# New instruction orders for all engines in the landmark-attention block of a two-block transformer kernel

## The chip, the cores and the metric

The kernel runs on one core of one Trainium2 chip. Its work is spread over the core's engines: TensorE (PE in the profile, with its weight loads as PEld), VectorE (DVE), ScalarE (ACT), GpSimd (POOL) and SyncE (SP), which issues most of the DMAs. The metric is the device time of one execution in microseconds (us); lower is better.

## The reference

Eight batches of 512 rows with 256 features pass through four layers, each added to its input after a layer norm:

```python
x = x + _L0_attn_a_ref(_layernorm(x), ...)   # cluster attention, 16 heads of 16
x = x + _L0_ffn_ref(_layernorm(x), ...)      # 8 experts, top 1, weighted by the softmax's maximum
x = x + _L0_attn_b_ref(_layernorm(x), ...)   # landmark attention, 64 landmarks
x = x + _L0_ffn_ref(_layernorm(x), ...)      # the same experts again
```

The landmark attention, with which the change deals, is this (its rows are seen as 8 batches of 512):

```python
q = q / scale
k_lm = k.reshape(Bb, H, m, Nn // m, hd).mean(axis=-2)
q_lm = q.reshape(Bb, H, m, Nn // m, hd).mean(axis=-2)
kernel1 = softmax(einsum('bhnd,bhmd->bhnm', q, k_lm))
kernel2 = softmax(einsum('bhld,bhmd->bhlm', q_lm, k_lm))
kernel3 = softmax(einsum('bhmd,bhnd->bhmn', q_lm, k))
SV = kernel1 @ iterative_inv(kernel2) @ (kernel3 @ v)
# iterative_inv: V = K.T / denom, then six times
#   KV = K @ V;  V = 0.25 * V @ (13 I - KV @ (15 I - KV @ (7 I - KV)))
```

The expert layer sends each row to one expert: a router gives the expert, a running sum gives the row's place in a table sorted by expert, the rows are scattered there, multiplied tile by tile with their expert's matrix, stored, gathered back and added.

## The kernel before

Everything is float32, and X (all 4096 rows) stays in SBUF. The program has two blocks that follow each other. The first, `cluster_attention`, does the cluster attention of batches 0 to 7 and the first expert layer of batches 0 to 3 (group `m0`), and begins that of batches 4 to 7 (group `m1`). The second, `landmark_attention`, does the landmark attention of batches 0 to 7, the rest of `m1`, and the second expert layer: group `m2` (batches 0 to 3), `m3` (batches 4 to 6), and `d7` (batch 7, which multiplies with all experts and so needs no scatter).

In each block every engine walks through a list of its own, a string of items in the tables `CLUSTER_ORDER` and `LANDMARK_ORDER`. An item is a batch (or group), a dot and a step; the code of a step stands once for each engine that takes part in it. Engines work strictly in the order of their lists and meet by semaphores, so an item whose input is late holds back all that stands behind it on its engine. An accumulator bank is handed out in the order in which TensorE claims it (six banks in a ring for the second block), so that the order of claims is also an order of waits.

The steps of a batch `n` in the second block, with the line of the profile where the text needs it:

- `xn`, `xT`, `q`, `k`, `v`: layer norm (DVE L1293), transposes (PE L1535), projections (PE L1540, L1546) and their copies by ACT. The layer norm's scales for batch 4 stand inside `4.xn` on DVE and wait for rows that `m1` has combined.
- `S2`, `e2`, `m2`, `kT`, `d`, `A`: kernel2, its softmax and the start of the inverse. `e2` is ACT L1443; `A` fills `b_aw`.
- `sc`, `ec`, `tc`, `w`: kernel3 by pairs of heads: scores (PE L1582), maximum (DVE L1350), exponential (ACT L1455), transposes and their copy (PE L1589, ACT L1460), product with v (PE L1596).
- `sa`, `ea`, `na`, `ta`: kernel1 in eight units: scores (PE L1610), maximum (DVE L1363) and a copy to SBUF (ACT L1470), subtraction (POOL L1247), exponential (ACT L1474), sum (DVE L1368) and division (POOL L1256), transposes (PE L1618) and their copy (ACT L1478).
- `R` and `N` with `U`, `Q`, `D`: the six rounds of the inverse, for all 16 heads at once in one pair of banks (`b_inverse`). `R` is the square KV (PE L1633), then DVE makes `b_uq` (L1379, L1388), ACT copies the square in three parts (L1498, L1505) and POOL subtracts (L1267, into `b_tm`); `N` is the second product (PE L1646) and DVE's update of `b_aw` (L1398). The rounds of one batch, and the batches behind each other, form one serial chain.
- `Z`, `sv`, `pj`: the inverse is applied (PE L1654, DVE L1407), multiplied with kernel1 (PE L1660, ACT L1507), projected (PE L1666), added to X and measured for the next layer norm (DVE L1416, L1418).
- `idle0`, `idle1`: three small products of the identity each (L1526 to L1528), whose results nobody reads.

The steps of a group: `ln`, `rn`, `rx`, `lg`, `lt` (norm, transposes, router logits), `c1`, `c2`, `s1` to `s4` on DVE (places; `s3` ends with `f_pos`, L403), `sc` on POOL (one indirect DMA per tile of 128 rows, L307), `ld` on SP (fetch), `tt` and `ty` (transposes and the product with the expert's matrix, PE L582 and L593), `st` (store), `ga` on POOL (one indirect DMA per tile, L318), `bi` (biases), `co` on DVE (combining, L455, which frees the row buffer that the sixth gather behind it needs).

Three lines say how a list is used and how a scatter waits:

```python
for n, item in plan["pool"]:
    body(item, n, n % 2 if isinstance(n, int) else None)
...
    if int(i) == 0:
        pool.wait_ge(self.s_clean, self.cleaned)
        self.placed.wait(pool, label)
```

## Time and profile before

| | us |
|---|---|
| median of three executions (lowest, highest) | 1116.17 (1111.09, 1122.37) |
| profiled execution, its own time | 1124.09 |
| span of that execution in the trace | 1121.9 |
| first instruction of the second block in the trace | 422.96 |
| mean granted TensorE clock, share of full speed | 0.925 |
| span of the second block | 699 |

The profiled execution took 2.2 us more than its span, which is what lies before the first and behind the last instruction, and 7.9 us more than the median. All that the change touches lies in the last 699 us of the span.

### The profile page before, as it was taken

The numbers are of one execution on the slowest core, as the hardware profiler recorded it, in microseconds if no ns is written. First come the engines' busy times: TensorE is split into PE (matmuls) and PEld (weight loads), VectorE is DVE, ScalarE is ACT, GpSimd is POOL, SyncE is SP. The second block draws the span as 40 slices with busy tenths as digits, with TensorE's granted clock in tenths as the row PEclk, the third lists the DMA queues.
The fourth block names the chain that finished last, engine by engine and source line by source line (L and its number), as shares of the span: only waits on it lengthen the run. The fifth ranks groups of instructions, "written<-read, shape, count | busy, mean of one in ns | idle before, by whom it ended". The sixth has DMA issues, their size and how long they took to land. (4 is left out here: it accounts for less than half of the span.)

```text
span 1121.9 us, 37263 instructions
## 1 busy us (share of the span) xinstructions
PE 933.2 (83%) x15213; PEld 666.9 (59%) x15213; DVE 831.1 (74%) x2089; ACT 641.6 (57%) x1387; POOL 472.3 (42%) x443
## 2 busy tenths in 40 slices
PE   7899989998989888677888986597689989772898
...
DMA packets 51079, 61.71 MB, mean 55 GB/s; under 512 B 5601, under 2 KB 46177, under 8 KB 50913
## 3 DMA queue, kind: packets, MB, share of 16 engines
...
## 5 line engine op out<-in xcount | busy, mean ns | idle before, releaser
L764 POOL TENSOR_TENSOR a_pr<-a_pr,a_smax 128x512 f32<-128x512 f32 x128 | 133.3, 1042 | 177.5 <-DVE a_smax L877 168.0
L1267 POOL TENSOR_TENSOR b_tm<-b_aw,b_sq 128x640 f32<-128x640 f32 (+1 forms) x48 | 65.4, 1362 | 148.9 <-ACT b_sq L1505 143.5
L871 DVE TENSOR_TENSOR a_pr<-a_bank,a_mask 128x512 f32<-128x512 f32 x128 | 82.8, 682 | 42.0 <-PE a_bank L1066 34.7
L963 ACT ACTIVATE a_pr<-a_pr 128x512 f32<-128x512 f32 x128 | 78.6, 630 | 51.9 <-POOL a_pr L764 44.1
L1247 POOL TENSOR_TENSOR b_pa<-b_pa,b_amax 128x512 f32<-128x512 f32 x64 | 67.1, 1048 | 70.3 <-ACT b_pa L1470 61.8
L969 ACT ACTIVATE a_pT<-a_bank 128x512 f32<-128x512 f32 x128 | 71.1, 596 | 41.2 <-PE a_bank L1075 30.0
L1075 PE MATMUL a_bank<-ident,a_pr 128*128 128x128 f32 x512 | 76.4, 289 | 20.2 <-ACT a_pr L963 17.6
L1256 POOL TENSOR_TENSOR b_pa<-b_pa,b_asum 128x512 f32<-128x512 f32 x64 | 66.7, 1043 | 58.4 <-DVE b_asum L1371 54.2
L307 POOL DMA_INDIRECT rows_sorted<-f_rows,f_pos x60 | 58.2, 969 | 72.2 <-DVE f_pos L403 53.8
L1398 DVE SCALAR_TENSOR_TENSOR b_aw<-b_tm,b_inverse 128x320 f32<-128x320 f32 (+1 forms) x144 | 63.4, 440 | 33.1 <-PE b_inverse L1646 13.7
L318 POOL DMA_INDIRECT f_rows<-results_sorted,f_pos x60 | 58.6, 977 | 66.9 <-issue 34.4
L877 DVE TENSOR_REDUCE a_smax<-a_pr 128x4 f32<-128x512 f32 x128 | 82.3, 675 | 0.4
L1075 PEld LDWEIGHTS a_bank<-ident,a_pr 128*128 128x128 f32 x512 | 60.2, 147 | 36.6 <-issue 34.2
L1633 PE MATMUL b_inverse<-b_aw 64*64 64x80 f32 x1536 | 44.8, 252 | 35.9 <-DVE b_aw L1398 26.9
L593 PE MATMUL b_bank<-experts_w,f_xgT 128*128 x260 | 69.5, 400 | 2.7 <-issue 1.7
L1646 PE MATMUL b_inverse<-b_uq,b_sq 64*64 64x80 f32 (+1 forms) x1536 | 40.2, 244 | 37.8 <-DVE b_uq L1388 35.9
L1633 PEld LDWEIGHTS b_inverse<-b_aw 64*64 64x64 f32 x1536 | 36.5, 146 | 50.9 <-issue 50.4
L1540 PE MATMUL b_bank<-b_xT,qkv_w 128*128 128x512 f32 x128 | 62.0, 626 | 3.2 <-ACT b_xT L1431 2.4
L1646 PEld LDWEIGHTS b_inverse<-b_uq,b_sq 64*64 64x64 f32 x1536 | 33.3, 144 | 51.1 <-issue 50.8
L1455 ACT ACTIVATE b_pc<-b_bank,b_nmax 128x512 f32<-128x512 f32 x64 | 43.4, 687 | 31.0 <-DVE b_nmax L1350 10.6
L1019 PE MATMUL a_bank<-a_xT,a_wqkT 128*128 128x512 f32 x128 | 59.9, 600 | 0.0
L1088 PE MATMUL a_bank<-a_V,a_pT 128*32 128x17 f32 x4096 | 48.7, 188 | 11.1 <-issue 10.9
...
## 6 DMA issues: line engine op xcount, KB each, us to landing
...
rows_sorted<-f_rows,f_pos POOLq DMA_INDIRECT x60
f_rows<-results_sorted,f_pos POOLq DMA_INDIRECT x60
```

What stands on the lines that cost most here:

```text
L593: last = mm(gb[:, 0:C], self.xgT[:, k % 3, kc, :], ew[:, kc, bass.ds(e, 1), :], start=(kc == 0), stop=(kc == 1))
L764: nc.gpsimd.tensor_tensor(out=pr[:, u % AHEAD], in0=pr[:, u % AHEAD], in1=smax[:, u % AHEAD, :].unsqueeze(2).broadcast_to([P, HQ, KEYS]), ...
L871: pre.emptied(V_.tensor_tensor(out=pr[:, u % AHEAD], in0=gb[:].rearrange("p (h k) -> p h k", h=HQ), in1=mask[:, u // 4, :].unsqueeze(1).br ...
L877: V_.tensor_reduce(out=smax[:, u % AHEAD, :], in_=pr[:, u % AHEAD], axis=AX.X, op=ALU.max)\
L963: nc.scalar.activation(pr[:, u % AHEAD], pr[:, u % AHEAD], ACT.Exp, scale=float(HD) ** -0.5)\
L969: pre.emptied(nc.scalar.activation(pT[:, u % TURNED], gb[:].rearrange("p (h q) -> p h q", h=HQ), ACT.Copy), n, item)
L1075: last = nc.tensor.transpose(gb[:, h * P:(h + 1) * P], pr[:, u % AHEAD, h, :], ident[:])
L1247: nc.gpsimd.tensor_tensor(out=p, in0=p, in1=amax[:, (n * NA + u) % AHEAD].unsqueeze(2).broadcast_to([P, H8, M]), op=ALU.subtract).then_inc ...
L1256: nc.gpsimd.tensor_tensor(out=p, in0=p, in1=asum[:, (n * NA + u) % AHEAD, 1].unsqueeze(2).broadcast_to([P, H8, M]), op=ALU.mult).then_inc( ...
L1267: nc.gpsimd.tensor_tensor(out=tm[:, a:b, k], in0=aw3[:, a:b, k], in1=sq[:, a:b, k], op=ALU.subtract).then_inc(s_tm, 1)
L1633: last = mm(products[lands(s, e), s, 0:AW], aw[r, par, s, 0:M], aw[r, par, s, :], start=True, stop=True)
L1646: last = mm(products[lands(s, e), s, k], sq[r, s, 0:M], uq[r, s, k], start=True, stop=True)
```

## The change

Only the table `LANDMARK_ORDER` is new; no step's code is touched, and the first block is as it was. Every engine has the same items as before, in another order. (The number of rows below differs by a few only because neighbours that are alike are shown as one.)
```diff
 LANDMARK_ORDER = {
     "pe": """
-        0.idle0 0.xT0 0.xT1 0.q0 0.k0 m1.rx3.0 0.q1 m1.rx3.1 0.k1 0.v0 0.v1 0.S20 0.S21 0.S22 m1.lg3 0.S23 0.idle1
...
+        0.xT0 0.xT1 0.q0 0.k0 0.q1 0.idle0 0.k1 0.idle1 0.v0 0.v1 m1.rx3.0 1.idle0 m1.rx3.1 0.S20 0.S21 0.S22 0.S23
...
```

**TensorE, from the end of batch 3 to the first products of batch 4.** Before:

```order
L1654 MATMUL b_bank<-b_aw,b_k2n 64x16 x16
L1660 MATMUL b_bank<-b_p1T,b_zbd 32x512 x8
L1666 MATMUL b_bank<-landmarks_proj,b_svT 128x256 x6
L1535 MATMUL b_bank<-ident,b_xn 128x128 x4
L1666 MATMUL b_bank<-landmarks_proj,b_svT 128x256 x2
L1535 MATMUL b_bank<-ident,b_xn 128x128 x4
L1540 MATMUL b_bank<-b_xT,qkv_w 128x512 x8
```

Now:

```order
L1654 MATMUL b_bank<-b_aw,b_k2n 64x16 x16
L1660 MATMUL b_bank<-b_p1T,b_zbd 32x512 x8
L1535 MATMUL b_bank<-ident,b_xn 128x128 x8
L1666 MATMUL b_bank<-landmarks_proj,b_svT 128x256 x8
L1540 MATMUL b_bank<-b_xT,qkv_w 128x512 x8
L1546 MATMUL b_bank<-qkv_w,b_xT 128x256 x8
```

The transposes of batch 4 stand ahead of batch 3's projection instead of in it and behind it.

**TensorE, around the place where the positions of group `m2` are computed** (L551 and L552 are `m2.s2`; L1633 is `4.R0`, L1646 `4.N0`). Before:

```order
L552 MATMUL b_bank<-f_total,experts_ones 128x8
L1596 MATMUL b_bank<-b_vv,b_p3T 32x16 x16
L1540 MATMUL b_bank<-b_xT,qkv_w 128x512 x2
L1596 MATMUL b_bank<-b_vv,b_p3T 32x16 x16
L1570 MATMUL b_bank<-b_k2T 64x64 x16
L1540 MATMUL b_bank<-b_xT,qkv_w 128x512 x2
L1618 MATMUL b_bank<-ident,b_pa 128x128 x12
L1546 MATMUL b_bank<-qkv_w,b_xT 128x256 x8
L1553 MATMUL b_bank<-b_klm,b_bdQ 128x64 x4
L1582 MATMUL b_bank<-b_kT,b_bdQ 128x512 x4
L1553 MATMUL b_bank<-b_klm,b_bdQ 128x64 x4
L1633 MATMUL b_inverse<-b_aw 64x80 x16
```

Now:

```order
L1570 MATMUL b_bank<-b_k2T 64x64 x16
L551 MATMUL b_bank<-f_total,experts_below 128x8
L552 MATMUL b_bank<-f_total,experts_ones 128x8
L1633 MATMUL b_inverse<-b_aw 64x80 x16
L1618 MATMUL b_bank<-ident,b_pa 128x128 x4
L1540 MATMUL b_bank<-b_xT,qkv_w 128x512 x8
L1546 MATMUL b_bank<-qkv_w,b_xT 128x256 x8
L1553 MATMUL b_bank<-b_klm,b_bdQ 128x64 x8
L1582 MATMUL b_bank<-b_kT,b_bdQ 128x512 x4
L1646 MATMUL b_inverse<-b_uq,b_sq 64x80 x16
```

The first square of batch 4 moved ahead of the projections of batch 5, which stood ahead of it. On POOL its `b_tm` moved from behind the 16 scatters to ahead of them, and in group `m3` the last gather of `m2` and 7.R0 both stand ahead of the 12 scatters (before, one gather was left behind them).

**ACT, from the end of batch 6 into batch 7 and the router of `m3`** (L1507 is `6.sv`, L1443 `7.e2`, L473 `m3.rn`, L484 `m3.rx`, L494 `m3.lg`). Before:

```order
L1443 ACTIVATE b_k<-b_k 128x512
L1507 ACTIVATE b_svT<-b_bank 128x512 x2
L1455 ACTIVATE b_pc,b_esum<-b_bank,b_nmax 128x512 x4
L1460 ACTIVATE b_p3T<-b_bank 128x512 x3
L473 ACTIVATE f_rows<-X,f_nbias,norm_rstd 128x256
L1460 ACTIVATE b_p3T<-b_bank 128x512
L473 ACTIVATE f_rows<-X,f_nbias,norm_rstd 128x256 x3
L1470 ACTIVATE b_pa<-b_bank 128x512 x2
L484 ACTIVATE f_xT<-b_bank 128x512 x2
L1470 ACTIVATE b_pa<-b_bank 128x512 x2
L494 ACTIVATE f_ex<-b_bank 128x128
```

Now:

```order
L1455 ACTIVATE b_pc,b_esum<-b_bank,b_nmax 128x512 x4
L1478 ACTIVATE b_p1T<-b_bank 128x2x2x128 x2
L1507 ACTIVATE b_svT<-b_bank 128x512 x2
L1470 ACTIVATE b_pa<-b_bank 128x512 x2
L1443 ACTIVATE b_k<-b_k 128x512
L1470 ACTIVATE b_pa<-b_bank 128x512 x2
L1474 ACTIVATE b_pa<-b_pa 128x512
L1460 ACTIVATE b_p3T<-b_bank 128x512 x2
L1474 ACTIVATE b_pa<-b_pa 128x512 x2
L1460 ACTIVATE b_p3T<-b_bank 128x512 x2
L473 ACTIVATE f_rows<-X,f_nbias,norm_rstd 128x256 x4
L1455 ACTIVATE b_pc,b_esum<-b_bank,b_nmax 128x512 x3
```

The four copies of kernel1's scores and its first three exponentials moved ahead of the router's first `rn`; before, all seven stood between the router's first `rn` and its last `lg`. One exponential (`7.ea3`) moved into that stretch.

At the block's start DVE's list has `0.q0` ahead of `m1.ln` (before, behind it), ACT's has the four `m1.rn` behind `0.k1` (before, three of them ahead of `0.q0`), and POOL's has ten scatters in a row, then `0.sa0` to `0.sa2`, `0.na0`, three scatters, `0.sa3`, `0.na1`, `0.na2`, three scatters, `0.na3` and then `0.R0` (before: five scatters, `0.sa0` to `0.sa3`, a scatter, `0.na0`, ten scatters, `0.R0`).

## Rows read from the trace of the kernel before

**Rows 1.** Busy time of each engine, from the page: us, share of the span, instructions.
```profile
PE 933.2 (83%) x15213; PEld 666.9 (59%) x15213; DVE 831.1 (74%) x2089; ACT 641.6 (57%) x1387; POOL 472.3 (42%) x443
```

**Rows 2.** Stretches of the second block: length, busy PE, PEld, DVE, ACT, POOL; clock; DMA.
```profile
423.00:456.00 33.00, 28.20 (x321) 18.95 (x321) 24.13 (x86) 14.98 (x32) 0.26 (x1) 1.00 0.04 11
456.00:488.00 32.00, 22.23 (x258) 14.16 (x258) 14.67 (x41) 14.81 (x31) 22.58 (x23) 0.88 0.19 67
488.00:698.00 210.00, 175.08 (x3163) 128.76 (x3163) 156.51 (x378) 139.35 (x307) 85.93 (x77) 0.95 0.11 34
698.00:736.00 38.00, 21.92 (x256) 16.05 (x253) 30.40 (x79) 11.17 (x22) 20.48 (x20) 0.60 0.14 39
...
788.00:811.00 23.00, 12.57 (x88) 9.41 (x86) 9.22 (x23) 7.59 (x17) 15.42 (x16) 0.71 0.28 94
811.00:963.00 152.00, 137.59 (x2422) 101.07 (x2419) 125.25 (x300) 107.56 (x242) 67.05 (x59) 0.97 0.14 42
963.00:985.00 22.00, 15.87 (x147) 10.03 (x146) 12.64 (x43) 6.89 (x17) 8.58 (x9) 0.77 0.20 56
985.00:1007.00 22.00, 17.90 (x405) 12.51 (x405) 17.51 (x52) 20.11 (x44) 12.08 (x12) 1.00 0.12 32
1007.00:1031.00 24.00, 6.11 (x137) 5.09 (x136) 13.98 (x39) 5.87 (x12) 14.73 (x15) 0.62 0.21 72
1031.00:1072.00 41.00, 35.13 (x459) 27.19 (x460) 20.01 (x49) 23.30 (x57) 16.92 (x15) 0.89 0.43 133
1072.00:1122.00 50.00, 43.60 (x148) 21.45 (x146) 31.19 (x85) 8.11 (x22) 11.41 (x12) 0.97 0.36 111
```

**Rows 3.** The chain that ended last, inside the 16 scatters of m2: start, us, what.
```profile
796.47 2.19 issue
...
806.04 1.11 issue
...
815.03 1.29 DVE b_amax L1363 x2
```

**Rows 4.** The same chain inside the 12 scatters of m3.
```profile
1017.93 2.83 another core or an unknown queue
...
1025.57 6.64 another core or an unknown queue
```

**Rows 5.** POOL in order of time, around three scatter runs: start, us, idle before.
```profile
456.09 1.01 POOL L307 DMA_INDIRECT rows_sorted<-f_rows,f_pos  x1 [32.83 <-DVE f_pos L403]
...
467.86 1.04 POOL L1247 TENSOR_TENSOR b_pa<-b_pa,b_amax 128x512 f32<-128x512 f32 x1 [2.54 <-ACT b_pa L1470]
...
486.13 1.54 POOL L1267 TENSOR_TENSOR b_tm<-b_aw,b_sq 128x640 f32<-128x640 f32 x1
...
788.09 1.03 POOL L307 DMA_INDIRECT rows_sorted<-f_rows,f_pos  x1 [6.50 <-DVE f_pos L403]
...
816.82 1.54 POOL L1267 TENSOR_TENSOR b_tm<-b_aw,b_sq 128x640 f32<-128x640 f32 x1 [8.73 <-ACT b_sq L1505]
...
1015.17 0.99 POOL L307 DMA_INDIRECT rows_sorted<-f_rows,f_pos  x1 [3.21 <-DVE f_pos L403]
```

**Rows 6.** All engines in order of time, end of batch 3 and start of batch 4.
```profile
720.30 1.38 DVE L1293 TENSOR_SCALAR b_xn<-X,norm_mean,norm_rstd 128x256 f32<-128x256 f32 x4
...
731.83 5.00 PE L1666 MATMUL b_bank<-landmarks_proj,b_svT 128*128 128x256 f32 x12 [0.80 <-ACT b_svT L1507]
...
739.35 3.24 PE L1540 MATMUL b_bank<-b_xT,qkv_w 128*128 128x512 f32 x7 [0.78 <-ACT b_xT L1431]
```

**Rows 7.** ACT's groups of instructions between 985 and 1007 us: busy us, mean ns.
```profile
L1460 ACT ACTIVATE b_p3T<-b_bank 128x512 f32<-128x512 f32 x6 | 3.4, 602 | 0.0
...
L1470 ACT ACTIVATE b_pa<-b_bank 128x512 f32<-128x512 f32 x4 | 2.2, 606 | 0.0
L1474 ACT ACTIVATE b_pa<-b_pa 128x512 f32<-128x512 f32 x3 | 1.9, 644 | 0.0
```

**Rows 8.** DVE's update of batch 0's first round, in order of time.
```profile
495.49 1.52 DVE L1398 SCALAR_TENSOR_TENSOR b_aw<-b_tm,b_inverse 128x320 f32<-128x320 f32 x3 [1.06 <-PE b_inverse L1646]
```

More of the change, by code:

```diff
@@ new lines @@
+        3.w2 3.w3 2.N3.0 3.m2 3.w4 3.sa0 3.sa1 3.sa2 3.sa3 2.R4.0 2.U4.0 3.d 3.w5 3.w6 2.N4.0 m1.bi0 m1.bi2 3.w7
+        m1.bi4 m1.bi6 2.R5.0 2.U5.0 3.na0 3.A 2.N5.0 3.na1 3.na2 3.R0.0 3.U0.0 m1.bi1 2.Z m1.bi3 3.N0.0 m1.bi5
+        m1.bi7 3.R1.0 3.U1.0 3.N1.0 3.sa4 3.sa5 3.sa6 3.R2.0 3.U2.0 3.N2.0 3.sa7 3.R3.0 2.pj0 3.U3.0 2.pj1 3.na3
+        3.N3.0 m1.co0 3.R4.0 3.U4.0 m1.co1 3.na4 3.na5 3.N4.0 m1.co2 3.na6 3.na7 3.R5.0 m1.co3 3.U5.0 4.xn 3.N5.0
+        2.pj2 2.pj3 3.Z m1.co4 m1.co5 m1.co6 3.pj0 m1.co7 m1.co8 m1.co9 3.pj1 3.pj2 3.pj3 m2.ln m1.co10 4.q0 4.k0
@@ new lines @@
+        5.sa0 5.sa1 4.N3.0 5.sa2 5.sa3 5.w4 4.na7 4.R4.0 4.U4.0 5.d 4.N4.0 4.R5.0 4.U5.0 5.A 5.w5 4.N5.0 4.Z 5.w6
+        5.w7 5.na0 5.na1 5.R0.0 5.U0.0 4.pj0 4.pj1 5.na2 4.pj2 4.pj3 6.q0 6.k0 6.q1 6.k1 6.sc0 6.sc1 6.sc2 6.sc3
+        5.N0.0 6.S20 6.S21 6.S22 6.S23 5.R1.0 5.U1.0 5.sa4 5.sa5 5.sa6 5.sa7 5.N1.0 7.xn 5.na3 6.w0 6.w1 5.na4
+        5.R2.0 6.sc4 6.sc5 6.sc6 6.sc7 5.U2.0 5.na5 5.na6 5.N2.0 6.w2 6.w3 6.m2 5.na7 6.w4 6.w5 5.R3.0 5.U3.0 6.d
+        5.N3.0 6.sa0 6.sa1 5.R4.0 6.sa2 5.U4.0 6.sa3 5.N4.0 6.w6 5.R5.0 5.U5.0 6.w7 6.A 5.N5.0 6.na0 6.na1 6.na2
@@ L1933 @@
+        m3.co6 d7.bi1 m3.co7 m3.co8 m3.co9 m3.co10 m3.co11 d7.dx2.0 d7.dx2.1 d7.dx2.2 d7.dx2.3 d7.dx3.0 d7.dx3.1
         d7.dx3.2 d7.dx3.3""",
     "act": """
[L1935 to L1937 removed]
@@ L1998 @@
[L1998 to L2005 removed]
+        m1.sc0 m1.sc1 m1.sc2 m1.sc3 m1.sc4 m1.sc5 m1.sc6 m1.sc7 m1.sc8 m1.sc9 0.sa0 0.sa1 0.sa2 0.na0 m1.sc10
@@ new lines @@
+        3.sa5 3.sa6 3.R4.0 3.sa7 m1.ga3 m1.ga4 3.na4 3.na5 m1.ga5 m1.ga6 3.R5.0 m1.ga7 3.na6 3.na7 m1.ga8 m1.ga9
+        m1.ga10 m1.ga11 m1.ga12 m1.ga13 m1.ga14 m1.ga15 4.sa0 4.sa1 4.sa2 4.sa3 4.na0 4.na1 4.na2 4.R0.0 m2.sc0
+        m2.sc1 m2.sc2 m2.sc3 m2.sc4 m2.sc5 m2.sc6 m2.sc7 m2.sc8 m2.sc9 m2.sc10 m2.sc11 m2.sc12 m2.sc13 m2.sc14
+        m2.sc15 4.sa4 4.sa5 4.na3 4.na4 4.sa6 4.R1.0 4.sa7 4.R2.0 4.na5 4.na6 4.R3.0 5.sa0 5.sa1 5.sa2 5.sa3 4.R4.0
+        4.na7 4.R5.0 5.na0 5.na1 5.na2 5.R0.0 5.R1.0 5.sa4 5.sa5 5.sa6 5.sa7 5.R2.0 5.na3 5.na4 5.na5 5.na6 5.na7
```

273 lines of the change are left out of this document (128 added, 145 removed).

## The prediction

> **What bounds the kernel now.** I read the busy times first, then the stretches of the second block, then the chain of waits and single engines in order of time at the places where a stretch is poor in work.
>
> No engine is full: TensorE has 83% of the span, VectorE 74%, the others less [rows 1]. The stretches of [rows 2] cover 647 of the block's 699 us, and in them TensorE is busy for 516, VectorE for 456, ScalarE for 360, POOL for 275. So the end of the block is set by order and waits, with TensorE nearest to being a bound. Two kinds of stretch differ. In the dense ones (488 to 698, 811 to 963) TensorE is busy for 83 and 91% at a clock of 0.95 and 0.97. In the poor ones it is not: 58% at 0.60 from 698 to 736, 55% at 0.71 from 788 to 811, 72% at 0.77 from 963 to 985, 25% at 0.62 from 1007 to 1031.
>
> Three of the poor places are scatter runs. POOL issues 16, 16 and 12 scatters, some 1.0 us busy each, as soon as `f_pos` is there: it had been idle for 6.50 us before those of `m2` and for 3.21 us before those of `m3` [rows 5]. While they go, POOL does nothing else, so the chain of the inverse (square, `b_tm` on POOL, second product, update) stands still if its POOL part is behind them. The chain of waits passes through this: "issue" of 2.19 and 1.11 us inside the run of `m2` [rows 3], and 2.83 and 6.64 us of a queue that the profile doesn't name inside that of `m3` [rows 4]. The other poor place is the end of batch 3: the layer norm of batch 4 is done at 720.30 + 1.38 = 721.7, but its transposes are in TensorE's group of twelve that begins at 731.83, behind part of batch 3's projection, and its first `q` is at 739.35 [rows 6].
>
> **The change part by part.** The items are the same, so nothing is removed or added; each term below is a place where an item waits on another one than before. I make the sum against the profiled execution, 1124.09 us, whose span is 2.2 us less, and carry the difference over to the median, 1116.17, 7.9 us below it. All of it lies in the block from 423 us on.
>
> *Start of the block.* `m1.ln` is now behind `0.q0` on VectorE and the `m1.rn` are behind `0.k1` on ScalarE. The group's positions, for which POOL's first scatter waits from the block's start [rows 5], thus come some 2 us later by my estimate (an item or two of about 1 us each on either engine). Ahead of `0.R0` on POOL stand now 16 scatters and eight other items (`0.sa0` to `0.sa3` with `0.na0` to `0.na3`), 24 in all, where there were 16 scatters and five, 21. Between the first scatter at 456.09 and `0.R0` at 486.13 lie 30.04 us [rows 5], of which 2.54 is a wait on `b_pa`; the rest over 21 or 22 items is 1.26 to 1.3 us each. Twenty-four give 30.2 us, and with 2 us of lateness and waits of the kind of the 2.54, `b_tm` may be ready up to 8 us later. What hides it is slack: `b_tm` was ready at 486.13 + 1.54 = 487.7, and VectorE's update that reads it began only at 495.49 [rows 8], 7.8 us later. So the cover is just enough, and once it is gone every microsecond costs one. I take +1, between −2 (the three `na` done early spare batch 0's kernel1 that much later on) and +8 (the update waits in full).
>
> *End of batch 3, start of batch 4.* The eight transposes now stand ahead of the eight products of `3.pj`. They can go in the wait for ScalarE's copies of `sv`, and the first `q` follows the projection at once. At best that takes away the group's own 5.00 us [rows 6]; at the least nothing, since the layer norm of `m2` needs `3.pj` as before, and now that comes behind the transposes. The gap between the group's end at 736.83 and `q` at 739.35 is 2.5 us; I take −2, since that gap is what the earlier transposes surely close. A half-speed clock in this stretch (0.60 [rows 2]) makes both parts longer but moves neither.
>
> *Batch 4 and the scatters of `m2`.* Before, `4.R0`'s square was done by 811 behind the projections of batch 5, and its `b_tm` on POOL came at 816.82, behind the 16 scatters, with 8.73 us of idle before it, for which ScalarE's copy of the square is named [rows 5]. Now the square is ahead of the projections and `b_tm` ahead of the scatters. Round 0 no longer waits for them, and N0 can run during the run. Round 1's `b_tm` still stands behind all 16, so no more than one round is gained. The upper bound of the gain is the 8.73 us of idle; on the other side, `b_tm`'s 1.54 us is now ahead of the scatters and, if `f_pos` is ready by then, delays them and all that follows by twice that much at most, +3. TensorE also gets the products of `m2.s2` later in its list than one square's worth. I take −4, about half of the bound, because batch 5's projections, moved behind the square, were work that TensorE did in that wait anyway.
>
> *Batches 6 and 7 and the scatters of `m3`.* Between 985 and 1007 ScalarE is busy for 20.1 of 22 us [rows 2], so here what stands in its list is time. Four copies of `b_pa` (2.2 us), three exponentials (1.9) and one copy of `b_p3T` (0.6) stood inside the router's steps and go ahead of them, one exponential (0.6) goes in: 4.1 us less [rows 7], in front of `f_pos`. POOL, however, has a gather (about 1.0) and `7.R0` (1.54) more ahead of the first scatter, at which it had idled for 3.21 us before: it is now free 0.7 us before the old start of 1015.17, and there the gain of 4.1 is cut down to 0.7. The 2.5 us of gather and `b_tm` then no longer stand behind the run. Together −3, between −5 (the 4.1 us in full and a part of the 2.83 [rows 4]) and +3 (the 2.5 us come on top because the copies of the square are late).
>
> *The dense stretches.* The six rounds of each batch are a chain; what surrounds them was reordered in many small ways which I can't price one by one. A gain there needs either a shorter round or a higher clock. I take 0, between −6 and +6, about 1.7% of their 362 us. The idle items are twelve times three small products before and after; they cost nothing where TensorE waits, and their new places are such.
>
> Sum: +1 − 2 − 4 − 3 + 0 = −8. The profiled execution would take 1116, the median 1108 us, 0.7% less.
>
> **The clock as a rival (faster).** By [rows 2], (1 − clock) × 2 × length is the time at the half level of 1.2 GHz: 7.7 us from 456 to 488, 21 from 488 to 698, 30.4 to 736, 13.3 from 788, 9.1 from 811, 10.1 from 963, 18.2 from 1007, 9 from 1031 and 3 at the end, 122 us together. Of these, 72 lie in the four poor stretches, where TensorE waits for others, and 39 in the dense ones and in 1031 to 1072, where its work is what one waits for. If the new order keeps TensorE busy more evenly, those 39 us go at the full clock and shrink by up to half, 19.5; I would expect two thirds of that, −13, on top of −8: 1095 us. For it speaks that the clock fell where TensorE paused, as before 736 and 1031; against it, that the idle items are as many as before and the pauses at the scatters stay. The Trainium skill, page "TensorE: Matmul & The Clock Gate", section "HAM oscillation — how this bites in real kernels", reckons the price as the throttled time times the half that the clock loses; by that rule all 122 us would be worth 61. The trace speaks against so much, since in 72 of them TensorE is busy for just over half of the time and is not what is waited for.
>
> **Later scatters as a rival (slower).** Steps of the chain and of kernel1 now stand ahead of or among the scatters on POOL. This costs nothing as long as POOL has done them before `f_pos` comes: the slack is 6.50 us at `m2`, 3.21 at `m3` and 7.8 at `0.R0` [rows 5, 8]. If inputs of these steps come late (each item waits in its place, as the 2.54 us did), the slack is used up and the whole scatter run, with fetch, product and gather behind it, moves. At the start that is +10 (24 items, 2 us of lateness and two waits of 2.5 us more, less the slack of 7.8, and behind it TensorE's `0.R1`, which stands behind `m1.tt0` in its list, by a scatter's fetch), at `m2` and `m3` +3 each; with the −2 at batch 4 and +1 of other waits, +15: 1131 us. The point from which it decides is `f_pos` being ready before POOL is.
>
> **A mere reshuffle as a rival (no change).** What the four places give is lost again at the next wait, since behind each comes a chain of rounds that is as long as before and a gather that waits for stores (963 to 985 is poor as well). That gives 1116 us.
>
> **How the numbers follow.** The forecast, 1108, has 0.38; its own bounds, the terms' ends taken partly together, go from −16 to 0, so that 0.14 of it is more than 1% faster. The clock has 0.24 and is all faster by over 1%. No change has 0.15. Later scatters have 0.18, slower by over 1%. For the rest, 0.05, I have no mechanism: 0.02 slower, 0.03 within. A difference of about 1% is what a measurement of this kernel can tell from none, as the three runs lie 1% apart. Faster 0.38, within 0.24 + 0.15 + 0.03 = 0.42, slower 0.20. The range from 1088 to 1128 holds the forecast, no change, the clock's case with 7 us to spare, and the milder third of the later scatters; outside are some 0.15 to 0.2.
>
> **What would show it.** In the trace of the changed kernel: the update of batch 0's first round not over 3 us after its old place, counted from the block's start (else the slack was less than I think); batch 4's first `q` about 2 us sooner behind `3.pj`; POOL's `4.R0` ahead of the first scatter of `m2` without a wait of its own for ScalarE, and the next `b_tm` directly behind the last scatter; the first scatter of `m3` with less than 1 us of idle before it; the granted clock of the dense stretches still 0.95 to 0.97, where the rival has 0.99. The prediction is wrong if the positions of a group are late by more than the slack, if a dense stretch of some 200 us differs by more than 6, or if the gathers' wait grows by what the scatters save.

## The result, and the profile after

The changed kernel takes 1134.48 us (median of four, 1131.78 to 1137.36) against 1118.73 (median of four). The ratio is 1.015, interval 1.0087 to 1.0214: slower, outside the range of 1088 to 1128 us that was forecast, and near the 1131 us of the rival with the later scatters.

The profiled execution has a span of 1130.0 us. Its page names the same busy times as [rows 1], with TensorE 6.6 us more:

```profile
PE 939.8 (83%) x15213; PEld 669.4 (59%) x15213; DVE 830.5 (73%) x2089; ACT 640.8 (57%) x1387; POOL 472.3 (42%) x443
```

The block takes 708.2 us here, 696.5 in the trace of before. Since times inside it shift, I cut it at marks, each the first instruction of an item on its engine: `0.xT0`, `0.Z`, `3.Z`, `4.q0`, the first scatter of `m2`, `4.R2`, `5.Z`, `7.R0`, the end. The rows of that view, columns as in [rows 2], for the changed kernel:

```profile
420.00:540.40 120.40, 96.22 (x1449) 66.50 (x1453) 79.11 (x220) 65.24 (x141) 42.01 (x40) 0.89 0.13 39
540.40:734.80 194.40, 155.95 (x2495) 109.92 (x2488) 139.95 (x344) 113.36 (x249) 82.20 (x75) 0.87 0.10 28
734.80:742.80 8.00, 7.26 (x73) 5.42 (x73) 5.80 (x15) 2.25 (x4) 3.33 (x5) 0.99 0.25 70
742.80:798.90 56.10, 46.38 (x603) 32.02 (x602) 47.03 (x152) 37.38 (x80) 11.85 (x12) 0.94 0.03 9
798.90:836.40 37.50, 23.46 (x276) 16.82 (x274) 22.74 (x58) 14.90 (x33) 23.27 (x23) 0.77 0.25 85
836.40:929.70 93.30, 84.92 (x1642) 64.61 (x1645) 71.81 (x178) 70.10 (x163) 37.16 (x33) 1.00 0.16 49
929.70:1018.40 88.70, 73.91 (x1106) 50.67 (x1098) 68.22 (x179) 53.41 (x115) 42.27 (x41) 0.88 0.11 32
1018.40:1128.20 109.80, 85.16 (x738) 54.70 (x737) 64.00 (x169) 37.11 (x91) 41.31 (x40) 0.84 0.35 114
```

And for the kernel before, in the trace of a control run (before_control below) on a chip with nearly the same times:

```profile
426.80:539.70 112.90, 86.64 (x1416) 61.79 (x1414) 76.99 (x220) 63.73 (x138) 42.21 (x40) 0.94 0.10 33
539.70:722.30 182.60, 145.31 (x2520) 106.08 (x2519) 140.94 (x343) 114.85 (x252) 79.34 (x72) 0.93 0.11 34
722.30:737.00 14.70, 8.96 (x72) 5.58 (x72) 9.88 (x27) 2.39 (x4) 7.43 (x8) 0.77 0.28 81
737.00:785.80 48.80, 40.98 (x548) 25.63 (x549) 41.63 (x137) 32.85 (x72) 8.24 (x8) 1.00 0.02 5
785.80:827.50 41.70, 26.50 (x386) 19.78 (x384) 26.48 (x65) 21.37 (x50) 23.91 (x23) 0.80 0.21 71
827.50:914.90 87.40, 80.59 (x1528) 61.09 (x1528) 70.29 (x174) 65.49 (x151) 36.59 (x33) 1.00 0.18 55
914.90:1002.00 87.10, 73.96 (x1141) 49.47 (x1141) 67.83 (x178) 54.91 (x119) 42.46 (x41) 0.96 0.10 31
1002.00:1114.80 112.80, 84.38 (x742) 53.24 (x741) 65.19 (x172) 37.33 (x91) 43.08 (x42) 0.86 0.35 112
```

So the loss has places, in us: the start (+7.5), batches 1 to 3 (+11.8), the way from `4.q0` to the first scatter (+7.3), batch 5 (+5.9). 5.Z to 7.R0 has +1.6. Three places gain: 3.Z to 4.q0 (−6.7), the scatters of `m2` (−4.2), the end (−3.0). Part of it is only shifted work: 1642 matmuls stand between `4.R2` and `5.Z` where 1528 stood, and 1106 for 1141 behind. These eight differences add up to 20.2 us, while the two spans differ by 13.4 (1130.0 and 1116.6): the first block, which is the same in both, happened to be 6.8 us shorter in the changed kernel's trace. Against the first trace of before, whose second block takes 696.5 us, the places are the same and the sizes differ: +4.6, +11.3, −8.9, +7.4, −6.3, +6.1, +0.8 and −3.3 in the order of the rows. One trace of a kernel is thus good for a place and not for the last few us of its size.

The first scatters and the `b_tm` around them, POOL in order of time in the changed kernel, answer to [rows 5]:

```profile
456.66 1.01 POOL L307 DMA_INDIRECT rows_sorted<-f_rows,f_pos  x1 [36.95 <-DVE f_pos L403]
...
480.56 1.04 POOL L1256 TENSOR_TENSOR b_pa<-b_pa,b_asum 128x512 f32<-128x512 f32 x1 [5.92 <-DVE b_asum L1371]
...
494.86 1.54 POOL L1267 TENSOR_TENSOR b_tm<-b_aw,b_sq 128x640 f32<-128x640 f32 x1
...
796.54 1.54 POOL L1267 TENSOR_TENSOR b_tm<-b_aw,b_sq 128x640 f32<-128x640 f32 x1 [9.00 <-ACT b_sq L1505]
798.89 1.03 POOL L307 DMA_INDIRECT rows_sorted<-f_rows,f_pos  x1 [0.81 <-DVE f_pos L403]
...
1026.63 1.00 POOL L307 DMA_INDIRECT rows_sorted<-f_rows,f_pos  x1 [2.39 <-DVE f_pos L403]
```

From the first scatter to `0.R0` it is 38.2 us (30.0 before), of which `0.na0` waits 5.92 us for its sums. At `m2` the idle time of 6.50 us in front of the scatters has become 9.00 in front of `b_tm` and 0.81 behind it. POOL now waits for the chain first, but that isn't what makes the scatters late: `b_tm` ends at 798.08 and `f_pos` only at 798.11.

### The profile page after: what moved, and what is told of

It is laid out like the page before. It is cut to its first block, busy times and chain, and to the rows that moved or that the text cites. A ratio compares the mean times of both kernels' runs of the same rounds, so it can differ in the third digit from the quotient of the medians.

```text
span 1130.0 us, 37271 instructions
## 1 busy us (share of the span) xinstructions
PE 939.8 (83%) x15213; PEld 669.4 (59%) x15213; DVE 830.5 (73%) x2089; ACT 640.8 (57%) x1387; POOL 472.3 (42%) x443
## 3 DMA queue, kind: packets, MB, share of 16 engines
q1 hardware_dynamic: 43584, 42.51, 11.8%
## 4 chain that ended last, share of the span: by engine, by line
PE 21%; DVE 14%; issue 6%; ACT 5%; POOL 4%; DMA 0%; SPq 0%; DVEq 0%; ACTq 0%; POOLq 0%
DVE b_aw L1398 3%; PE b_bank L593 2%; PE b_bank L1540 2%; PE b_bank L570 2%; PE b_bank L1666 2%; PE b_inverse L1646 1%; DVE b_amax L1363 1%; PE b_bank L1660 1%; POOL b_tm L1267 1%; PE b_bank L1618 1%; DVE b_nmax L1350 1%; DVE b_uq L1388 1%; DVE b_asum L1368 1%; PE b_inverse L1633 1%; POOL rows_sorted L307 1%
## 5 line engine op out<-in xcount | busy, mean ns | idle before, releaser
L1633 PE MATMUL b_inverse<-b_aw 64*64 64x80 f32 x1536 | 41.7, 251 | 30.9 <-DVE b_aw L1398 28.3
L1646 PE MATMUL b_inverse<-b_uq,b_sq 64*64 64x80 f32 (+1 forms) x1536 | 42.4, 244 | 28.8 <-DVE b_uq L1388 16.3
L1633 PEld LDWEIGHTS b_inverse<-b_aw 64*64 64x64 f32 x1536 | 34.2, 145 | 45.3 <-issue 45.1
L1491 ACT ACTIVATE b_aw<-b_aw 128x640 f32<-128x640 f32 (+1 forms) x48 | 32.2, 670 | 49.8 <-DVE b_aw L1398 47.6
L1646 PEld LDWEIGHTS b_inverse<-b_uq,b_sq 64*64 64x64 f32 x1536 | 34.5, 144 | 43.1 <-issue 42.8
L1470 ACT ACTIVATE b_pa<-b_bank 128x512 f32<-128x512 f32 x64 | 37.0, 599 | 38.9 <-DVE b_amax L1363 18.2
```

Source lines behind the costliest of these rows:

```text
L1633: last = mm(products[lands(s, e), s, 0:AW], aw[r, par, s, 0:M], aw[r, par, s, :], start=True, stop=True)
L1646: last = mm(products[lands(s, e), s, k], sq[r, s, 0:M], uq[r, s, k], start=True, stop=True)
```

## The experiments

The chips differ: before_control, before_two_pieces, router_first and the pieces start, mid and tail ran on chips on which the kernel before takes 1116 to 1123 us, as in the result above (group 1), all others where it takes 1081 to 1085 (group 2). Every ratio is to the kernel before on the same chip, so that over 1 is slower, with its 95% interval in brackets. A "piece" is the table of one kernel in which, between two times of its own trace, every engine's items stand in the other kernel's order; a diff shows the first items that differ in TensorE's list. Where the two orders are joined there is a seam.

**start** (one piece of the new order in the kernel before), here POOL's list:

```diff
-m1.sc0 .. m1.sc4 0.sa0 0.sa1 0.sa2 0.sa3 m1.sc5 0.na0 m1.sc6 .. m1.sc15 0.R0.0 0.na1 0.na2
+m1.sc0 .. m1.sc9 0.sa0 0.sa1 0.sa2 0.na0 m1.sc10 .. m1.sc12 0.sa3 0.na1 0.na2 m1.sc13 .. m1.sc15 0.R0.0
```

> The kernel before, but every engine has the changed kernel's order for the items of the block's start (those that the trace of before shows before 497.3 us, which ends with the scatters of m1 and 0.R0 on POOL). Theory 1, each piece costs where it stands: the trace of the changed kernel has 0.N0 5.3 us later than before and 0.Z 4.6 us later, counted from the block's start, so this kernel is 4 to 6 us slower (ratio 1.004 to 1.005). Theory 2, late tiles: the first fetch of m1 is 11 us later (m1.ld0), TensorE's list meets the tiles in batches 1 to 3, and this piece alone brings most of the 16 us that 3.Z is late: 10 to 16 us slower (1.009 to 1.014).

Measured 1.0051 (1.0021 to 1.0082). `0.Z` stands at 116.5 us from the block's start (111.2 to 112.9 in four traces of group 1 with the old start, 115.8 in that of before), and at `3.Z` the lag is still that: 0.Z to 3.Z takes 184.9 us, 182.6 to 185.1 in the others, although the first fetch of `m1` is 13 us late (76.8 us from the block's start, against 62.9 to 63.9). So late tiles hold nothing up, and theory 1 holds.

**rounds_1_to_3** (batches 0 to 3 behind the start):

```diff
-0.R1.0 1.w0 1.w1 m1.tt0 m1.tt1 m1.ty0 1.tc2 1.tc3 1.kT 0.N1.0
+0.ta3 2.xT0 1.w0 m1.tt0 0.R1.0 1.tc2 1.w1 1.w2 m1.tt1 1.tc3
```

> The kernel before, with the changed order only for the items between 498.5 and 722 us of its trace (rounds 1 to 5 of batch 0, batches 1 to 3 and the tiles of m1). The scatters of m1 keep their old place, so the tiles are not late. Theory 1, the order of the dense stretch itself is worse: of the 11.4 us that 3.Z lost between 0.Z and 3.Z in the changed kernel most are lost here too, ratio 1.006 to 1.011, and 3.Z stands 8 to 13 us behind the traces of the kernels that keep the old order here. Theory 2, late tiles: no more than 3 us, ratio 1.000 to 1.003. The three other pieces gave 1.0051, 1.0018 and 1.0058, which leaves 1.002 for this one if the ratios add up to the whole, 1.015.

Measured 1.0105 (1.0059 to 1.0151). With tiles on time 0.Z to 3.Z takes 191.2 us, 184.4 to 184.8 with the old order in group 2. This is theory 1: the order of the stretch itself is worse.

**mid** (end of batch 3 to `4.R2`):

```diff
-3.pj0 3.pj1 3.pj2 4.xT0 3.pj3 4.xT1 4.q0 4.k0 4.q1 4.k1 m2.rx0.0
+4.xT0 4.xT1 3.pj0 3.pj1 3.pj2 3.pj3 4.q0 4.k0 4.q1 4.k1 4.v0 4.v1
```

> The kernel before, with the changed order only for the items between 722 and 830 us of its trace (3.pj, the transposes of batch 4, batch 4 up to its second round, the positions and scatters of m2). In the changed kernel the lag at 3.Z, 16.0 us, was 8.2 us at 4.R2. Both theories: 5 to 8 us faster (0.993 to 0.996) if that gain belongs to the order. A rival, that a late stretch merely catches up (work that was ready earlier because the batch before was late): no gain, 1.000.

Measured 1.0018 (0.9986 to 1.0051): no gain. Its parts, though, are there: 3.Z to 4.q0 takes 13.5 us (14.7 to 16.9 in the others), the first scatter to 4.R2 40.0 (41.7 to 44.9), and in between the 57.9 us from 4.q0 to the first scatter, instead of 48.8, eat both.

**tail** (from `4.R2` on):

```diff
-m2.tt3 m2.tt4 4.R2.0 5.tc4 m2.ty2 5.tc5 4.ta3 6.xT0 6.xT1 m2.tt5
+4.idle0 6.xT0 6.xT1 4.R2.0 m2.ty2 4.N2.0 4.ta3 4.ta4 m2.tt3 m2.tt4
```

> The kernel before, with the changed order only from 830 us of its trace on (batches 4 to 7 from the second round of batch 4, the tiles of m2, router and scatters of m3, the end). Lag in the changed kernel 8.2 us at 4.R2, 14.2 at 5.Z, 11.7 at the end. If it belongs to the order: 3.5 us slower (1.003), with 5.Z 6 us late and 2.5 given back at the end. If it comes from the state that the middle leaves behind: 0.

Measured 1.0058 (1.0027 to 1.0090); 4.R2 to 5.Z takes 91.8 us (87.1 to 88.1 in the others), and from there to the end 198.2 (198.1 to 201.0). The loss belongs to the order; the 2.5 us that were expected back at the end can't be told from the spread. The four pieces multiply to 1.023, where the whole has 1.015 and, in group 2, 1.0112 (after_again below); with intervals of 0.003 to 0.005 each that may be noise or the seams.

**xt_first** (kernel before, the one change that I had priced at −2):

```diff
-pe:  3.pj0 3.pj1 3.pj2 4.xT0 3.pj3 4.xT1
+pe:  4.xT0 4.xT1 3.pj0 3.pj1 3.pj2 3.pj3
-dve: m1.co7 m1.co8 3.pj0
+dve: 3.pj0 m1.co7 m1.co8
```

> The kernel before with the transposes of batch 4 (4.xT0, 4.xT1) ahead of 3.pj0 on TensorE, and 3.pj0 ahead of m1.co7 and m1.co8 on VectorE; nothing else. In the trace of the middle piece 4.q0 comes 13.5 us after 3.Z, where it is 16.9 in the traces with the old order. If this is worth what it seems, 3 us faster (0.997), and all marks behind 4.q0 come 3 us sooner. Rival: m2.ln, which waits for 3.pj3, becomes late as it did in the middle piece, and by the first scatter of m2 nothing is left: 1.000.

Measured 1.0004 (0.9968 to 1.0039). 3.Z to 4.q0 takes 10.9 us for 14.1 in before_again, 4.q0 to the first scatter 51.3 for 48.8: of 3.2 us 0.7 arrive, which timing can't show. The rival was right.

**after_ln_first** and **after_noidle** (changed kernel):

```diff
-dve: 0.xn 0.q0 m1.ln            act: 0.q0 ... 0.k1 m1.rn12 m1.rn13 m1.rn14 m1.rn15
+dve: 0.xn m1.ln 0.q0            act: m1.rn12 m1.rn13 m1.rn14 0.q0 m1.rn15
```
```diff
-pe:  0.idle0 0.idle1 1.idle0 ... 5.idle1
```

> The changed kernel with one thing put back: m1.ln ahead of 0.q0 on VectorE, and the four m1.rn around 0.q0 on ScalarE as before. In the changed kernel VectorE is idle for 6.6 us between 0.xn and 0.q0, where m1.ln (3.2 us) stood before, and the first scatter of m1 is 4.2 us late. Theory 1a, the lateness of f_pos is what the start costs: the first scatter comes back to 32 to 33 us from the block's start, and the kernel is 4 us faster than the changed one (1.011 against before). Theory 1b, the interleaving on POOL costs it (the run of scatters took 36 us in place of 29): the first scatter comes back but 0.N0 stays late, and the gain is under 2 us (1.013 to 1.015).

> The changed kernel without the twelve idle items (36 small products of the identity, whose results nobody reads; they only keep TensorE busy). If the clock theory holds, the granted clock of the first 120 us of the block falls below 0.89 and the kernel is slower than the changed one, 1.018 or more. If they do nothing where they stand: 1.015, clock the same within 0.01. If they are in the way (seven of them stand in TensorE's list while it has work for the positions of m1): 1.011 to 1.013.

Measured 1.0139 (1.0091 to 1.0187) and 1.0160 (1.0109 to 1.0211). Without idle items the clock of the first 109 us is 0.87, where the six other traces of group 2 that start in the new order have 0.89 to 0.94. It isn't that one trace alone: over six executions each, on one chip, the mean granted clock is 0.927 without the idle items and 0.939 in after_ln_first, which has them. So they seem to lift the clock (the two kernels differ in `m1.ln` as well). The time doesn't follow: the means are 1094.8 and 1092.8 us, 2.0 apart with a noise of 4. They neither help nor harm by more than the 0.5% that this shows. after_ln_first has its first scatter at 33.0 us, but after_noidle at 32.5 and squares_first below at 33.0 as well, so that can't be put down to `m1.ln`.

**before_again, after_again, after_rounds_old, after_mid_old**: the two kernels unchanged, and the changed one with the old order in one piece each:

```diff
-after_rounds_old: 0.sa4 1.tc1 2.xT0 1.w0 m1.tt0 0.R1.0 3.idle0
+after_rounds_old: 3.idle0 1.tc1 0.sa4 0.R1.0 1.w0 1.w1 m1.tt0
-after_mid_old: 4.xT0 4.xT1 3.pj0 3.pj1 3.pj2 3.pj3 4.q0
+after_mid_old: 3.pj0 3.pj1 3.pj2 4.xT0 3.pj3 4.xT1 4.q0
```

> The kernel before, unchanged, as a control with a profile of its own on the chip on which the three kernels beside it run. Ratio 1.000 within 0.004. The marks of its trace, counted from the block's start, are what the others are held against: if the stages are as repeatable as they look (the same order gave the same length of a dense round within 0.2 us in five traces), they agree with the first trace outside the scatter runs.

> The changed kernel once more, unchanged, on the same chip as the control. Ratio 1.010 to 1.020. On the other chip the kernels with the changed start (without idle items, or with m1.ln put back) had their first scatter at 32.5 to 33.0 us and 0.Z at 109 us from the block's start, 5 us sooner than the old order there; on the first chip the changed kernel had 36.7 and 120.4. If that difference is the chip's, the changed kernel has 0.Z at about 109 here (or 120, if this is the first chip).

> The changed kernel with the old order of the items between 496 and 735 us of its trace (batch 0 from its first round on, batches 1 to 3, the tiles of m1, and the first items behind). Theory 1 (the dense stretch's own order costs 7 to 11 us): 1.005 to 1.009 against before, that is 6 to 10 us faster than the changed kernel. Rival, that the stretch only shifts work (TensorE has 86 more matmuls between 0.Z and 2.Z and 3.pj follows 3.Z 7.5 us sooner): under 3 us, 1.012 to 1.016.

> The changed kernel with the old order of the items between 735 and 829 us of its trace (3.pj, batch 4 up to its first rounds, positions and scatters of m2). The middle piece alone gave 1.0018 and its trace was 9 us later between 4.q0 and the first scatter of m2 and 3.4 and 3.8 us sooner on either side. So 0 to 2 us faster than the changed kernel: 1.013 to 1.015. If the late positions of m2 matter more in the changed kernel than alone (5.Z stood 14 us late): 1.010 or less.

Measured 0.9958 (0.9920 to 0.9997), 1.0112 (1.0061 to 1.0163), 1.0037 (1.0004 to 1.0069) and 1.0079 (1.0045 to 1.0113). The first says how far a ratio can be trusted: a kernel against itself is 0.4% off. Taking back the rounds gives back 0.75% (7.1 us between the means, with a noise of 3.6), which is clear. Taking back the middle gives back 0.3% (3.3 us), which isn't. Lengths in us between marks, where the traces of group 2 have the one or the other order there, with the number of traces:

| | old order | new order |
|---|---|---|
| start to 0.Z | 111.3, 114.0 | 108.8 to 115.2 (7 traces) |
| 0.Z to 3.Z | 184.4 to 184.8 (3) | 190.9 to 194.6 (7) |
| 3.Z to 4.q0 | 14.1 (10.9 in xt_first) | 7.9 (6) |
| 4.q0 to first scatter of m2 | 48.7 to 48.8 (3) | 56.1 to 57.0 (6) |
| first scatter to 4.R2 | 32.9 to 33.0 (3) | 30.8 to 31.6 (6) |
| 4.R2 to 5.Z | 87.2 to 89.0 (3) | 93.3 to 93.7 (7) |
| 5.Z to 7.R0 | 78.9 to 81.4 (3) | 76.5 to 78.3 (7) |
| 7.R0 to the end | 106.4 to 108.2 (3) | 105.1 to 107.9 (7) |

(positions_first is left out behind 4.q0, chain_first between 0.Z and 3.Z, and so are lengths with the seam of a piece in them.) From 3.Z to 5.Z the same order takes nearly the same time in every kernel of group 2; over 0.Z to 3.Z it varies by 3.7 us and over the start by 6.4, with the same order there. The upper ends of the old order from 4.R2 on (89.0, 81.4, 108.2) are all from before_again, whose profiled execution took 1089.25 us, 7.5 over its median. In group 1 the start costs (116.5, 120.4 and 125.7 against 111.2 to 115.8), in group 2 these lengths show no cost. Work has also moved over the marks, so neighbouring rows belong together: from 0.Z to 4.q0 it is 199.0 us in after_again, 198.6 in before_again and 195.3 in xt_first, which has the early transposes of batch 4 as well; from 4.R2 to 7.R0 170.1, 170.4 and 166.1.

**squares_first** and **chain_first** (changed kernel), one of the moves each:

```diff
-act: 1.Q3.0 2.ec4 2.ec5 2.ec6 2.ec7 1.R3.0
+act: 1.Q3.0 1.R3.0 2.ec4 2.ec5 2.ec6 2.ec7
-dve: 2.S22 2.S23 2.sc0 2.sc1 2.sc2 2.sc3 1.N1.0
+dve: 2.S22 1.N1.0 2.S23 2.sc0 2.sc1 2.sc2 2.sc3
```

> The changed kernel; in ScalarE's list of batches 1 and 2 seven copies of the square (1.R0, 1.R1, 1.R2, 1.R3, 1.R5, 2.R2, 2.R4) are moved ahead of the 2 to 8 items that stood between them and the moment at which the square is ready. In the trace of the changed kernel these copies begin 14.4 us (batch 1, six rounds together) and 16.1 us (batch 2) after their squares, in the control 4.0 and 14.0. Theory, the copies that stand behind other work are what makes batch 1 longer: 1.Z and 2.Z come 5 to 9 us sooner, ratio to the changed kernel 0.993 to 0.996 (1.004 to 1.009 against before). Rival, VectorE's update or TensorE's list is late anyway: under 2 us.

> As squares_first, and on VectorE too: the parts of the rounds of batches 1 and 2 (b_uq of a round and the update of b_aw) stand where they become ready, ahead of the maxima, sums and w items (1 to 5 of them) that were ahead of them. VectorE's update began 11.0 us late in batch 1 and 8.8 in batch 2. Theory: another 5 us at 2.Z, 8 to 14 us together, ratio to before 1.000 to 1.006. Rival, that what is moved behind (maxima of kernel3, by which ScalarE and TensorE go on) becomes late in its turn: not better than squares_first, 3.Z where it was.

Measured 1.0099 (1.0064 to 1.0135) and 1.0198 (1.0150 to 1.0246), where after_again has 1.0112. By its ratio squares_first could still be at the edge of its forecast, 1.009; the lengths decide, and the theory falls in both runs. The copy of the square moves to where it should be, and yet 0.Z to 2.Z stays at 145.7 us; with VectorE's part moved too it grows. That stretch in xt_first (old order), after_again, squares_first and chain_first:

```profile
526.80:664.80 138.00, 119.87 (x2019) 85.73 (x2022) 100.71 (x247) 93.06 (x209) 50.47 (x45) 0.96 0.11 35
```
```profile
527.90:674.00 146.10, 123.81 (x2016) 86.66 (x2007) 103.31 (x255) 93.40 (x210) 52.38 (x48) 0.96 0.09 29
```
```profile
522.20:667.90 145.70, 125.23 (x2013) 87.38 (x2002) 103.26 (x255) 93.05 (x210) 52.32 (x48) 0.95 0.09 29
```
```profile
529.40:686.50 157.10, 131.49 (x2014) 90.87 (x2007) 104.94 (x255) 92.26 (x209) 52.04 (x48) 0.90 0.09 27
```

Between the first two, with as many matmuls, TensorE is 3.9 us longer busy and 4.2 longer idle. In the last one the clock falls to 0.90, and busy time takes 7.7 of the 11.0 us more (its profiled execution, 1109.73 us, was the longest of its six, so its row may overstate both). What TensorE waited for between 0.Z and 4.q0 (line, waited for, us in total, times, longest), first before_again, then after_again:

```profile
PE b_inverse L1633 <- DVE b_aw L1398: 16.0, 12, 3.1
PE b_inverse L1646 <- DVE b_uq L1388: 10.9, 9, 2.6
```
```profile
PE b_inverse L1633 <- DVE b_aw L1398: 12.4, 8, 3.9
PE b_inverse L1646 <- DVE b_uq L1388: 5.9, 7, 2.5
PE b_bank L1618 <- POOL b_pa L1256: 5.3, 4, 2.3
PE b_bank L582 <- ACT b_pc L1455: 2.9, 4, 1.7
```

The waits for the chain fell by 8.6 us. Waits of kernel1's and the experts' transposes (8.2 us), which the old order hardly had, took their place.

**positions_first** (changed kernel, batch 4 and the positions of `m2`):

```diff
-pe:   4.A m2.s2 4.R0.0                              pool: 4.R0.0 m2.sc0 .. m2.sc4
+pe:   m2.s2 4.A 4.R0.0                              pool: m2.sc0 .. m2.sc4 4.R0.0
-dve:  4.d 4.A m2.s1 4.R0.0 m2.s2 m2.s3
+dve:  m2.s1 m2.s2 m2.s3 4.d 4.A 4.R0.0
```

> The changed kernel with the positions of m2 ahead of batch 4's chain: on VectorE 4.d, 4.A and 4.R0 behind m2.s3, on TensorE m2.s2 ahead of 4.A, on POOL 4.R0 behind the fifth scatter. In the changed kernel the first scatter of m2 is 56.1 us behind 4.q0, before 48.8; of the 7.3 us 1.7 are 4.d and 4.A, 0.5 is 4.R0, and 1.2 is m2.s3, which takes 2.3 us instead of 1.1 while POOL works on 4.R0. Theory: the first scatter comes 3 to 4 us sooner (52 to 53), m2.s3 is back at 1.1 us, and the kernel is 1 to 3 us faster than the changed one, the rest being that the group's router itself is late. Rival: the first scatter comes sooner but 4.N0 later by as much, and nothing is gained.

Measured 1.0105 (1.0062 to 1.0148). The first scatter comes 52.5 us behind 4.q0, as expected, and the way from there to 4.R2 is 35.0 us in place of 31.0, so that nothing is left: the rival was right. The last step of `m2.s3`, in the changed kernel and in positions_first:

```profile
796.76 1.35 DVE L403 CAST f_pos<-f_posf 128x16 int32<-128x16 f32 x1
```
```profile
781.44 0.17 DVE L403 CAST f_pos<-f_posf 128x16 int32<-128x16 f32 x1
```

**before_chain_first** (kernel before and xt_first, 54 moves of the kind of chain_first; one of them):

```diff
-dve: 1.pj0 1.pj1 1.pj2 1.pj3 2.R1.0 2.U1.0
+dve: 2.R1.0 1.pj0 1.pj1 1.pj2 1.pj3 2.U1.0
```

> A candidate that may beat both: the kernel before, with the transposes of batch 4 first (as xt_first), and in all eight batches ScalarE's copies of the square and VectorE's parts of a round moved ahead of what stood between them and their becoming ready (54 moves of 1 to 7 places). If the chain of rounds is the backbone everywhere, 8 to 15 us faster (0.986 to 0.993). If the other work that is displaced bounds the dense stretches (TensorE is busy for 83 to 91% there), between 0.996 and 1.004.

Measured 1.0148 (1.0105 to 1.0192): slower than either forecast. 4.R2 to 5.Z takes 95.6 us for 87.2 to 89.0. "Chain first", applied as in these two runs, makes either kernel slower.

**router_first** (changed kernel), **before_two_pieces**, **before_control** (the kernel before):

```diff
-router_first: pe: 4.k1 4.v0 4.v1 m2.rx0.0 m2.rx0.1 m2.lg0 4.sc0 m2.lt0
+router_first: pe: 4.k1 m2.rx0.0 m2.rx0.1 m2.lg0 4.sc0 4.v0 m2.lt0 4.v1
-router_first: act: m2.rn13 4.ea1 4.ea2 4.tc4 4.ea3 m2.rn14 m2.rn15
+router_first: act: m2.rn13 m2.rn14 m2.rn15 4.ea1 4.ea2 4.tc4 4.ea3
-before_two_pieces: pe: 6.R1.0 6.sa4 m2.ty19 m2.tt21 6.N1.0 (xt_first besides)
+before_two_pieces: pe: 4.idle0 4.idle1 7.xT0 7.xT1 6.R1.0 6.sa4 6.N1.0
```

> The changed kernel with the router of m2 moved ahead in two places: TensorE's 4.v0 and 4.v1 behind m2.lg0 (in the changed order ahead of m2.rx0.0), their copies with them on ScalarE, and ScalarE's m2.rn14 and m2.rn15 ahead of 4.ea1, 4.ea2, 4.tc4 and 4.ea3. In the changed kernel the last router product m2.lg3 is 43.1 us behind 4.q0 (before 35.5), the first scatter 56.1 (48.8), and TensorE then waits once for 5.3 us at m2.tt0, which it did not before. Theory, this lateness is what the middle costs: the first scatter at 52 to 54, the wait at m2.tt0 below 3 us, 1 to 3 us faster than the changed kernel. Rival: positions_first showed that scatters 3.6 us sooner give nothing by 4.R2 when batch 4 pays for them; here too the kernel's time is the changed kernel's.

> A candidate for a kernel that beats both: the kernel before with the transposes of batch 4 first (as xt_first) and the changed order only from 927 us of its trace on (batches 6 and 7, router and scatters of m3, the end). These are the two pieces in which the traces of one chip show the new order ahead: 3.4 us at 4.q0, and 3.2 us between 5.Z and the end (185 us in the changed kernel, 188 to 190 in the others). If both last: 5 to 7 us faster, 0.994 to 0.996; if neither does: 1.000.

> The kernel before, unchanged, as a control beside them: 1.000 within 0.004, and its marks are what the candidate's are held against.

Measured 1.0136 (1.0086 to 1.0186), 1.0057 (1.0021 to 1.0094) and 0.9970 (0.9927 to 1.0012). With the router moved the way to the first scatter is 56.1 us, to the tenth what it was, and so is the place of the last router product, 43.0 us behind 4.q0 in both traces: the move brought the first products forward and not the last one, and the transpose behind that one waits 0.58 us for VectorE's `b_aw` in both. So the move doesn't reach what sets the positions. By the trace it is VectorE, and positions_first, which took three of VectorE's items out of the way, agrees. In the changed kernel it is busy from the end of `5.xn` (782.6) to the end of `m2.s3` (798.1) with one pause, before `4.d`:

```profile
791.16 0.69 DVE L1334 TENSOR_REDUCE b_dmax<-b_bank 128x8 f32<-128x512 f32 x1 [0.53 <-PE b_bank L1557]
...
794.03 0.48 DVE L1379 SCALAR_TENSOR_TENSOR b_uq<-b_aw,b_inverse 128x320 f32<-128x320 f32 x1
```

These 15.5 us are 10.0 in before_control (775.0 to 785.0). `4.m2` (1.6 us), `4.w4` to `4.w7` (1.5), `4.A` (0.8) and `4.R0` (0.5) stand in between now and didn't before, and 1.2 is the cast above; `5.xn` itself ends 1.8 us later behind 4.q0. The two pieces don't gain together either: 5.Z to 7.R0 takes 93.8 us (86.8 to 87.9). The seam stands in that stretch and is the likely cause, which no run tests. No kernel that I tried is faster than the one before.

## Why the prediction was wrong, step by step

**The dense stretches**, "I take 0, between −6 and +6", is the step that failed. What I put at nothing measures +6.7 us between 0.Z and 3.Z in group 2 (11.3 to 11.8 in group 1) and 5 to 6 between 4.R2 and 5.Z in both, 12 to 13 together in group 2, of which 3.Z to 4.q0 and 5.Z to 7.R0 give back 2 to 4 each because work was moved (in group 1 only the former does). With the moved work counted in, and against xt_first, that leaves 3.7 us from 0.Z to 4.q0 and 4.0 from 4.R2 to 7.R0. In the time rounds_1_to_3 shows it with 1.0105 and after_rounds_old with 0.75% less; tail has 0.6% more, little over the 0.4% that a kernel differs from itself. The sign that I had given for being wrong, a stretch of some 200 us that differs by more than 6, came true with 11.8. I had reasoned that a gain there needs a shorter round or a higher clock and left the loss at a like size; but in a stretch that is 83 to 91% full any item placed before its input is there stops TensorE's whole list. Which items do so I know by the waits alone. In batches 1 and 2 they aren't simply the chain's parts behind other work: squares_first and chain_first show that.

**Batch 4 and the scatters**, −4 with +3 as the other bound. The gain is there (4.2 us in the pair of traces above, 2.0 in group 2), and the bound on the other side was too small: the first scatter is 7.3 us later behind 4.q0, in both groups, so the two together cost 3.1 us in that pair and 5.4 in group 2. In the time mid (1.0018) and after_mid_old (0.3%) don't show it clearly. I had counted `b_tm`'s 1.54 us on POOL and not what precedes it on VectorE. positions_first shows that some half of it is batch 4's chain ahead of the positions, and that either order pays the same by 4.R2. The check that I gave, "without a wait of its own for ScalarE", is wrong: the wait is 9.00 us. The stall also didn't go away in group 1: during the scatters TensorE creeps through whichever product stands there, the square before and the second product now. Rows of the waits between 4.q0 and 4.R2, before_control, then the changed kernel:

```profile
PE b_inverse L1633 <- issue: 8.1, 7, 1.8
```
```profile
PE b_inverse L1646 <- issue: 8.0, 8, 1.8
```

In group 2 it doesn't creep, but in after_again TensorE waits once at the transposes of the first tile, which it didn't in before_again:

```profile
PE b_bank L582 <- issue: 5.3, 1, 5.3
```

**The start**, +1 within −2 to +8. `0.R0` is 12.4 us later from the block's start (8 foreseen), the update of `0.N0` 5.3, against "not over 3", and start has 0.5%: the upper half of the bounds. In group 2 no trace shows a cost.

**End of batch 3**, −2: 14.1 to 10.9 us in xt_first, 16.9 to 13.5 in mid. Right, and worth next to nothing in time, as the rival in xt_first says. **`m3`**, −3: 5.Z to the end is 198.5 us, 199.9 in before_control; in group 2 it is 181.6 to 185.9 in seven traces with the new order, and 185.5, 185.5 and 189.6 with the old, the last that of before_again. Near in size, though not clear of the spread; and the first scatter still waits 2.39 us, where I expected under 1.

**The clock.** The rival's sign was wrong. By the rows above, (1 − clock) × 2 × length sums to 158 us at the half level of 1.2 GHz in the changed kernel and 101 in before_control; TensorE is busy for 573.3 and 547.3 us, 26 more, and idle for 6 less. So in these two traces of group 1 the difference is in the clock. The Trainium skill, "TensorE: Matmul & The Clock Gate", section "HAM oscillation — how this bites in real kernels", values throttled time at half of it: by that estimate 57 us more would be worth 28, and the pair agrees with 26. The pair flatters the rule, though: before_control's profiled execution has the highest clock (0.945) of the twelve of its run. Against the first trace of before, whose TensorE is busy for 559 us of the block, busy time is 14 us more, where the blocks differ by 11.7.

For group 2 a pair of traces can't settle it, since before_again's was taken in an execution that was slow for this kernel (clock 0.939, where the others average 0.948), after_again's in the one with the highest clock of its six. The means over the executions of one chip, from which the ratios are formed, say more:

| | mean time, us | mean granted clock |
|---|---|---|
| before (28 executions) | 1084.0 | 0.945 |
| after_again (6) | 1094.7 | 0.937 |
| after_rounds_old (12) | 1087.6 | 0.932 |

From the first row to the second the loss and a lower clock go together. From the second to the third they don't: with the old rounds the kernel is 7.1 us faster at a clock that is no higher. Nor do they in after_noidle, 0.012 lower at the same time. The mean clock counts the half level in pauses, too, and a pause in which TensorE waits for others gets no longer by it (my reading), so the mean clock can't price an order. The dense stretches have 0.94 (0.Z to 2.Z) and 1.00 (4.R2 to 5.Z) in the changed kernel, where I had expected 0.95 to 0.97. The clock falls where the order makes pauses: between 2.Z and 3.Z it is 0.64 to 0.69 in every trace with the new order there and 0.74 to 0.78 with the old. How the loss divides into pauses and clock on one chip stays open, as does why the new start costs time in group 1 alone.

**Later scatters**, the rival at 0.18 with 1131 us, came nearest: +10 at the start was 7.5 (4.6 against the first trace of before), +3 at `m2` was 7.3, `m3` nothing (8.2 us from 7.R0 to the first scatter in both). That its 1131 is so near to 1134 is partly luck, as it left out the dense stretches, and what it gave to the start isn't there in group 2, where the kernel is slower all the same.
